# The causal mask's two constant tiles in bf16 instead of fp32r

## The reference

```python
x = _layernorm(x + _L0_attn_ref(x, ...))            # causal self attention
x = _layernorm(x + _L0_xattn_ref(x, ctx_768, ...))  # attention over the 1024 context rows
x = _layernorm(x + _L0_ffn_ref(x, ...))             # soft mixture of 8 experts
x = _layernorm(x + _L1_attn_ref(x, ...))            # causal self attention
x = _layernorm(x + _L1_xattn_ref(x, ctx_768, ...))
x = _layernorm(x + _L1_ffn_ref(x, ...))             # causal self attention again, then routed experts, 2 of 8
```

```python
w = jnp.einsum('bhnd,bhmd->bhnm', q, k) * jax.lax.rsqrt(float(D))
mask = jnp.tril(jnp.ones((S, S), dtype=jnp.float32))
w = jnp.where(mask > 0, w, NEG)
w = jax.nn.softmax(w, axis=-1)
attn = jnp.einsum('bhnm,bhmd->bhnd', w, v)
```

## Time and profile before

| | |
|---|---|
| median of 3 runs | 2791.5 us (2788.26 to 2793.62) |
| the profiled execution | 2784.09 us |
| its span, first to last instruction | 2782.3 us |
| outside the span | 1.8 us |
| PE busy | 2507.6 us, 90% of the span |
| weight loads (PEld) busy | 1434.3 us, 52% |
| DVE busy | 1495.4 us, 54% |
| ScalarE (ACT) busy | 1326.7 us, 48% |
| GpSimd (POOL) busy | 455.7 us, 16% |
| mean granted clock of PE | 0.957 |

### The profile page before, as it was taken

How to read it: one execution, slowest core, us unless ns; L and a number is a source line. 1 busy time by engine, 2 the same in 40 slices (tenths; PEclk the granted TensorE clock), 3 DMA queues, 4 the chain that set the end, 5 groups by cost and what they waited for, 6 DMA issues and landing times. The chain is left out here.

```text
span 2782.3 us, 47352 instructions
## 1 busy us (share of the span) xinstructions
PE 2507.6 (90%) x15751; PEld 1434.3 (52%) x15752; DVE 1495.4 (54%) x4204; ACT 1326.7 (48%) x2826; POOL 455.7 (16%) x735
## 2 busy tenths in 40 slices
PE   6999999999979889999699999999998988599991
PEld 3555544444444456676355544444445555367661
DVE  2555777888644500013455688878756664322224
ACT  2655466677754521211355556666675544122220
POOL 4233212101100000000113312122121122120004
PEclk8999999999999999999799999999999988699995
DMA  7555534232800022203654452332422454111103
GB/s 224 159 142 142 144 92 110 54 80 62 260 1 1 1 97 89 72 12 137 189 141 142 135 131 67 84 103 62 109 67 90 138 159 161 67 63 32 34 30 97
DMA packets 156895, 276.78 MB, mean 99 GB/s; under 512 B 22928, under 2 KB 98960, under 8 KB 152208
## 3 DMA queue, kind: packets, MB, share of 16 engines
q1 hardware_dynamic: 152896, 262.56, 33.0%
q0 software_dynamic: 3792, 11.54, 1.3%
HBM read 195.51 MB, written 95.29 MB: 105 GB/s over the span
## 5 line engine op out<-in xcount | busy, mean ns | idle before, releaser
L1634 ACT ACTIVATE second_p<-psum 128x512 f32<-128x512 f32 (+3 forms) x1024 | 462.1, 521 | 264.6 <-PE psum L1435 251.9
L1634 ACT ACTIVATE first_p<-psum 128x512 f32<-128x512 f32 (+3 forms) x768 | 366.7, 548 | 163.7 <-PE psum L1435 160.4
L1732 DVE TENSOR_REDUCE second_max_parts<-psum 128x1 f32<-128x512 f32 x512 | 322.7, 684 | 68.7 <-PE psum L1412 64.8
L1732 DVE TENSOR_REDUCE first_max_parts<-psum 128x1 f32<-128x512 f32 x512 | 322.9, 684 | 61.7 <-PE psum L1412 59.2
L1728 DVE CUSTOM_DVE_ANT_0 second_masked<-psum,mask_qk 128x384 f32<-128x384 f32 (+3 forms) x512 | 229.7, 489 | 192.7 <-PE psum L1412 163.4
L1447 PE MATMUL psum<-second_p,second_v_aug 128*32 128x512 f32 (+3 forms) x2048 | 235.5, 532 | 5.5 <-ACT second_p L1634 4.8
L1425 PE MATMUL psum<-second_q,second_k 64*128 64x512 f32 (+3 forms) x1024 | 225.4, 436 | 6.9 <-DVE second_max_parts L1728 4.5
L1412 PE MATMUL psum<-second_k,second_q 64*128 64x512 f32 (+3 forms) x1024 | 199.8, 387 | 30.4 <-DMA second_k<-a_k_parts 13.6
L1435 PE MATMUL psum<-second_shift_T,choose 64*128 64x512 f32 (+3 forms) x1024 | 197.6, 381 | 0.0
L1425 PEld LDWEIGHTS psum<-second_q,second_k 64*128 64x128 f32 x1024 | 97.8, 186 | 189.5 <-ACT second_p L1634 81.0
L2511 ACT ACTIVATE routed_space<-psum,routed_bias 128x128 f32<-128x128 f32 x312 | 84.9, 383 | 214.5 <-PE psum L2436 214.5
(11 more groups left out here) (341 smaller groups left out, 3865.4 us busy)
## 6 DMA issues: line engine op xcount, KB each, us to landing
first_k<-c_k_parts SPq DMA_DIRECT2D x64, 256.0 KB, 4.7
second_q<-a_q_parts SPq DMA_DIRECT2D x128, 128.0 KB, 3.0
second_k<-a_k_parts SPq DMA_DIRECT2D x128, 128.0 KB, 3.0
second_k<-c_k_parts SPq DMA_DIRECT2D x64, 256.0 KB, 4.8
first_q<-a_q_parts SPq DMA_DIRECT2D x64, 128.0 KB, 3.2
first_k<-a_k_parts SPq DMA_DIRECT2D x64, 128.0 KB, 3.1
c_k_parts<-first_held SPq DMA_DIRECT2D x16, 512.0 KB, 3.1
first_q<-c_q_parts SPq DMA_DIRECT2D x64, 128.0 KB, 4.3
```

Source lines behind the costliest of these rows:

```text
L1634: evacuated(act.activation(probs[tile % 2][:, 2 * h + p, q0:SEQ], bank[:, q0:SEQ], ACT.Exp, scale=scale), event)
L1732: evacuated(v.reduce_max(max_parts[n % 2][:, h, p, qt, k0 // BANK:k0 // BANK + 1], bank[:, 0:width], axis=AX_X), event)
```

## The change

Both tiles of the mask product, the stationary `pick` and the streaming `mask_kq`, are allocated as bf16 instead of fp32r. Their values are the same, as far as bf16 holds them; their sources were bf16 already. On no engine does an instruction move, come or go. DVE's eight copies of L159 write bf16 instead of fp32r.

```diff
@@ -110,10 +110,10 @@
     c.x_tok = c.keep("x_tok", [P, NT, D])
     c.ident = c.keep("ident", [P, P])
     c.ident_bf = c.keep("ident_bf", [P, P], BF16)
-    c.pick = c.keep("pick", [P, 2, P], F32R)
+    c.pick = c.keep("pick", [P, 2, P], BF16)
     c.choose = c.keep("choose", [P, 2, P], F32R)
     c.mask_qk = c.keep("mask_qk", [P, SEQ])
-    c.mask_kq = c.keep("mask_kq", [P, 2, P], F32R)
+    c.mask_kq = c.keep("mask_kq", [P, 2, P], BF16)
     c.eps = c.keep("eps", [P, 1])
```

## The result

The changed kernel takes 2767.12 us in the median of 4 runs (2757.77 to 2770.92), the kernel before 2790.36 us beside it: 23.2 us less, ratio 0.9911 with a 95% interval of 0.9884 to 0.9937. The forecast was 2762 us, in a range of 2750 to 2793.

A forecast was written before the change was run, and what follows sets the result against it. PE, busy 90% of the span, was taken as the bound in the self layers; 288 x 0.08 + 96 x 0.14 = 36.5 us on PE, 30.4 us passed on, took 2791.5 us to 2762 us, range 2750 to 2793.

The forecast's parts named there:

- The bound and the mechanism: Self layers: other engines wait for PE; loads run one step ahead, so short mask products cannot cover fp32r loads of 0.11 us.
- The load's time: The `pick` loads of the masks: a bf16 load takes at most 0.03 us in the queue, against 0.11 us for fp32r.
- the gain of an event: Self-layer score events on PE: 0.08 us less for 256 queries and more, 0.14 us for 128; 36.5 us in sum.
- The share that arrives: Self layers: 0.83 of the PE gain reaches the end, so 36.5 becomes 30.4 us.
- the 0.9 for the first two layers: First two self layers: 0.9 of the PE gain is passed on to the kernel's time.
- The signs that it named for this case: Too much passed on: events shorten but stretches do not, and idle time before L1425's loads, put down to ScalarE or DVE, grows.
- Nothing gained: Mask loads: bf16 in 64-row tiles still takes 0.11 us, so the time stays 2791 us; chance 0.12.
- Slower, by the change of type: Score events: the array empties at each switch between fp32r and bf16, 54 to 65 us slower, about 2850 us; chance 0.18.
- later than 0.28 us: 384-query events: if the first masks (L1431) start more than 0.28 us behind L1425, types cost something.
- Half the gain: Mask loads: the two halves load one after the other or at 0.055 us, 22.4 us gained, 2769 us; chance 0.17.
- full gain: Mask loads of at most 0.03 us: 30 us gained, 2762 us, own range 2752 to 2770; chance 0.53.
- The casts and the addresses: Eight copies now writing bf16, and later tiles moved by 1 KB in each partition: both put at nothing.

The follow-up runs named there:

- one-pair runs: One pair of mask products in place of two per event: kernel before 2742.21 us (0.9904), changed kernel 2740.8 us (0.9899).
- run with 96 columns: Changed kernel with `pick` cut to its first 96 columns, the mask of each tile's last 32 keys left out: 2750.92 us (0.9917).
- run with the filler: Changed kernel with a same-size filler behind each bf16 tile, so later tiles keep their addresses from before the change: 2749.81 us against 2772.1 (0.9917).

## Why the prediction was right, and what was off

**The bound and the mechanism held.** The gain is in the loads, it is on PE, and it stands in the self layers alone. The one-pair runs carry this most: nothing between the types with one pair in the sum of the events and 1.4 us in the times, and 22 to 23 us with two, is what a queue of loads, one ahead, gives, and a product that is cheaper by itself does not. That 2767 lies in the range says less, since 2750 to 2793 holds every case from no gain to the full one.

**The load's time** was put at 0.03 us at most, on the low side of its bounds, and rightly: the second masks follow the first by 0.039 us for 64 columns (0.027 us) in the medians, 0.012 for the load. The 32 cycles that the prediction took from the Trainium skill ("TensorE: Matmul & The Clock Gate", Weight-path perf modes) stand in its table beside fp8, and its measured gain there is about 2x; the 27 ns are an estimate for another type, and the sum did not need them.

**The term that was mis-sized** is the gain of an event, 0.08 us for 256 queries and more and 0.14 for 128. It measured 0.066 and 0.118, 30.4 us for 36.5. The step had the first masks loaded ahead of L1425's end, as the fp32r ones had been, and nothing between the masks. In fact both loads stand in the open: the first masks start 0.285 us behind L1425 in place of 0.280, the second 0.039 behind these in place of 0.030, 0.014 us together. In events of 128 queries they start 0.168 and another 0.041 us on, where the prediction had 0.16 and 0.03. That is the difference of 0.08 and 0.066, and most of that of 0.14 and 0.118. No row before the change shows a bf16 load behind an fp32r stream in one tile shape; whether it runs ahead should have been bounded, and was assumed.

**The share that arrives** was chosen as 0.83 and is 0.73 to 0.76 in three measurements. How it splits can be read from the shift products of successive groups, whose loads (L1466) give the first and last start in a stretch; 14 groups or 112 events lie between, worth 112 x 0.079 = 8.9 us on PE. First self layer, then the second, of the kernel before:

```profile
L1466 PEld LDWEIGHTS psum<-ident_bf,first_shift x60: 95/98/99, 77.3 to 325.4; 128*128 128x128 bf16 x60
...
L1466 PEld LDWEIGHTS psum<-ident_bf,second_shift x60: 95/98/99, 1384.7 to 1635.5; 128*128 128x128 bf16 x60
```

of the changed kernel:

```profile
L1466 PEld LDWEIGHTS psum<-ident_bf,first_shift x60: 95/98/99, 78.4 to 321.3; 128*128 128x128 bf16 x60
...
L1466 PEld LDWEIGHTS psum<-ident_bf,second_shift x60: 95/98/99, 1384.2 to 1629.3; 128*128 128x128 bf16 x60
```

and of its second profile, the first self layer:

```profile
L1466 PEld LDWEIGHTS psum<-ident_bf,first_shift x60: 95/98/99, 76.2 to 317.2; 128*128 128x128 bf16 x60
```

The first layer went from 248.1 to 242.9 us, 5.2 of 8.9. In the second profile, from another chip, it is 241.0, 7.1 of 8.9 or 0.8; the second profile of the kernel before has 249.7. Part of the difference is the clock: from 215 to 230 us it was granted at 1.00 before and 0.89 after, the share that the page counts, with a short stretch at the low level of 1.2 GHz that the second profile does not have. The last but two number of this row is that clock.

```profile
215.00:230.00 15.00, 13.48 (x108) 8.17 (x108) 7.13 (x32) 7.73 (x17) 1.96 (x2) 0.89 0.46 141
```

The rest is waits: the loads of L1425 now wait for ScalarE's copy of the shift (L1645) at the start of seven groups. This line, from 78.4 to 321.3 us, has none to answer to it before, where such waits were nothing or too short for the view:

```profile
PEld psum L1425 <- ACT first_shift_T L1645: 1.7, 7, 0.2
```

The second layer gave 5.7 of 8.9, 0.64, with a clock of 1.00 in both. There too the waits grew, by about the 3.2 us that are missing: the loads of L1425 wait 2.1 us more for the exponentials, those of L1412 0.9 and 0.6 us more for DVE. From 1384.7 to 1635.5 us before and from 1384.2 to 1629.3 us after:

```profile
PEld psum L1425 <- ACT second_p L1634: 4.6, 8, 0.7
PEld psum L1412 <- DVE second_max_parts L1732: 3.8, 6, 0.9
PEld psum L1412 <- DVE second_max_parts L1728: 2.7, 8, 0.5
```

```profile
PEld psum L1425 <- ACT second_p L1634: 6.7, 14, 0.8
PEld psum L1412 <- DVE second_max_parts L1732: 4.7, 9, 1.0
PEld psum L1412 <- DVE second_max_parts L1728: 3.3, 8, 0.5
```

The two groups ahead of this stretch gained nothing: PE waits there for the context's transfer until 1369.8 us before and 1369.9 after, and what the two groups save, 16 x 0.079 = 1.3 us, goes into that wait:

```profile
PE psum L1582 <- DMA routed_up<-in_ctxT: 6.6, 1, 6.6
...
PE psum L1582 <- DMA routed_up<-in_ctxT: 7.9, 1, 7.9
```

So the 0.9 for the first two layers was too much, and more so in the second. The prediction had the first self stretch 11 us shorter; the 14 groups of it are 5 to 7 us shorter. The signs that it named for this case came: the events shortened by more than the stretches, and idle time before the loads of L1425 grew.

In the third layer the clock changes level many times. Fourteen groups of it take 234.5 us (from 2096.2 on) and, in the second profile, 229.3 before, and 226.7 after, at clocks of 0.90, 0.92 and 0.91, so the gain can't be read there. In the second profile of the changed kernel they take 208.1 at 0.97: most of the 18 us between the chips lies in this layer.

In the cross layers six groups after the second self layer take 163.1 us both times, from 1635.4 to 1798.5 us before and from 1629.2 to 1792.3 us after. In the first cross layer the clock cost something. One group of it, before and after:

```profile
470.40:504.10 33.70, 25.86 (x176) 11.23 (x173) 28.38 (x67) 18.53 (x35) 4.47 (x16) 0.95 0.23 55
...
466.10:502.90 36.80, 29.07 (x177) 12.55 (x173) 28.74 (x67) 18.53 (x35) 4.46 (x16) 0.81 0.21 50
```

The same work takes 3.1 us more at 0.81 in place of 0.95, and 36.6 us at 0.82 in the second profile of the changed kernel; the second profile of the kernel before has 35.6 at 0.86. So 1 to 3 us of the gain were lost here in these profiles; whether the change brings that on, two profiles of each can't show.

The share falls with size, as such waits would have it: 0.76 for the change, 0.71 for one fp32r pair gone, 0.62 for all masks gone (53 of 85 us), 0.55 for what lies between the two. Of work added to the kernel before, 0.76 arrives (65.5 of 85.7 us). Why of the bf16 pairs added to the changed kernel only 0.54 does (17.5 of 32.1) stays open; the two times are known to some 3 and 5.5 us either way. That it is waits that make the share fall with size is argued here; no run tests it.

**The rivals.** "Nothing gained" fell: the bf16 loads of 64 rows have 96 ns in the records, as those of 128 rows have 98. "Slower, by the change of type" fell too: the bf16 masks start 0.285 us behind a 384-query L1425 where the fp32r ones started 0.280 behind it, and the run with 96 columns has bf16 loads ahead of an fp32r stream and its first masks at 0.280. By the letter of the prediction's sign ("later than 0.28 us") the 0.285 would mean a cost of the type; it is the load. "Half the gain", 2769 us, is nearest to 2767 as a number, by another way: the load is as fast as in the full gain, and what is missing is 0.014 us an event and the share.

**The casts and the addresses** cost nothing: the run with the filler gives the same, and the copies of L159 end at 5.2 us, before `choose` waits 2.04 us for GpSimd.

The runs of one kernel spread with the clock: the four of the result have 2757.77 us at a mean granted clock of 0.959 and 2770.92 at 0.954, so a profile of one run can be off by half of this gain.

## What to carry to other kernels

In this kernel a short fp32r product on PE costs its weight load, not its columns, as soon as the one before it is short too, because only one load is done ahead: read the distances between the starts of the loads, and count the loads that no stream covers. Making such a load cheaper pays where two or more stand in a row, and with one behind a long stream it pays nothing; then look at the next load behind them, which here (`choose`) was worth 16 to 19 us more. Take a share off for waits on other engines. When you compare waits of two profiles, take the stretches between the same instructions, not between the same times: the work has moved.

## What the runs showed of the hardware

A 128-column bf16 load costs 0.005 to 0.012 us in the open and is not done ahead of an fp32r stream (it starts 0.28 us behind L1425's load in an event of 384 queries, and that of a bf16 `choose` 0.33 us behind a 512-query L1425), whereas a 96-column bf16 load is (0.11 us behind it), and fp32r loads are. The Trainium skill ("TensorE: Matmul & The Clock Gate", LDWEIGHTS) has the load's time as columns over 1.2 GHz; the fp32r pairs agree with 0.11 us, the bf16 pairs do not. The Trainium skill ("TensorE: Matmul & The Clock Gate", Weight-path perf modes) gives the fast load only to 128 weights of a type other than FP32, and the 96-column loads, longer at 119 ns in the records than the 96 ns of the 128-column ones, agree with that.

Going from fp32r to bf16 and back within the same tile shape showed no cost of its own: the first bf16 masks start 0.285 us behind a 384-query L1425, the fp32r ones 0.280, and bf16 ones of 96 columns, which load ahead, 0.280 too.
